# Two layers on one core: VectorE's order of sums and maxima in the units of the first layer's attention

## The reference

```python
Q = (x @ Wq.T + bq).reshape(B, S, H, dk)      # B=32, S=256, H=16, dk=8
K = ...; V = ...
scores = jnp.einsum('bqhd,bkhd->hbqk', Q, K)
attn = jax.nn.softmax(scores, axis=1)         # over b, the 32 sequences
heads = jnp.einsum('hbqk,bkhd->bqhd', attn, V)
```

## Time and profile before

| what | value |
|---|---|
| median of 3 runs | 1535.37 us (1533.78 to 1540.93) |
| the profiled execution, its own time | 1537.03 us |
| its span, first to last instruction | 1535.3 us |
| TensorE busy | 1345.0 us (88%) |
| VectorE busy | 1063.1 us (69%) |
| ScalarE busy | 821.2 us (53%) |
| GpSimd busy | 1045.2 us (68%) |
| VectorE's maxima (L847) | 128 of 2282 ns each |
| VectorE's sums (L865) | 128 of 2276 ns each |

### The profile page before, as it was taken

How to read it: one execution, slowest core, us unless ns; L and a number is a source line. 1 busy time by engine, 2 the same in 40 slices (tenths; PEclk the granted TensorE clock), 3 DMA queues, 4 the chain that set the end, 5 groups by cost and what they waited for, 6 DMA issues and landing times. The chain is left out here.

```text
span 1535.3 us, 41490 instructions
## 1 busy us (share of the span) xinstructions
PE 1345.0 (88%) x14592; PEld 1057.5 (69%) x14593; DVE 1063.1 (69%) x1847; ACT 821.2 (53%) x1820; POOL 1045.2 (68%) x763
## 2 busy tenths in 40 slices
PE   6867999999999999996699968989999699999960
PEld 4635666666666666664589966776777699999960
DVE  5638999999999999998656535756744333333329
ACT  7824777777777777775234425533344244444430
POOL 6734999999999999999344435477777444444430
PEclk9969999999999999999699979999999899999985
DMA  6876233433333443313254431011111122222228
GB/s 215 296 216 164 71 92 95 99 97 94 95 99 98 99 100 100 93 30 130 76 159 144 146 106 56 22 51 58 41 44 44 46 67 67 66 65 65 66 86 286
DMA packets 112207, 155.16 MB, mean 101 GB/s; under 512 B 17856, under 2 KB 85696, under 8 KB 107200
## 3 DMA queue, kind: packets, MB, share of 16 engines
q1 hardware_dynamic: 78496, 106.64, 25.5%
q0 software_dynamic: 13344, 27.92, 5.5%
q10 hardware_dynamic: 20224, 18.65, 3.8%
HBM read 95.33 MB, written 57.82 MB: 100 GB/s over the span
## 5 line engine op out<-in xcount | busy, mean ns | idle before, releaser
L1035 POOL TENSOR_TENSOR V<-Ex,R 128x4096 f32<-128x4096 f32 x64 | 477.3, 7458 | 14.8 <-ACT R L955 14.7
L964 ACT ACTIVATE Ex<-pB 128x512 f32<-128x512 f32 x512 | 305.2, 596 | 115.1 <-PE pB L754 96.7
L847 DVE TENSOR_REDUCE mg<-pA 128x128 f32<-128x2048 f32 x128 | 292.1, 2282 | 9.4 <-PE pA L734 9.4
L865 DVE TENSOR_REDUCE Z<-Ex 128x64 f32<-128x2048 f32 x128 | 291.0, 2276 | 7.2 <-ACT Ex L964 7.2
L1120 POOL DMA_INDIRECT y_d<-x1yb,x1xb x136 | 131.6, 968 | 151.4 <-DVE x1yb L1257 144.9
L764 PE MATMUL pO<-V,Vh 128*8 128x128 f32 x4096 | 161.8, 279 | 14.1 <-POOL V L1035 14.1
L1797 POOL DMA_INDIRECT xs_d<-d_xn,d_idx x128 | 130.9, 1023 | 42.1 <-issue 35.3
L1257 DVE COPY x1yb<-x1pY 128x128 f32<-128x128 f32 x136 | 39.7, 292 | 161.2 <-PE x1pY L1154 161.2
L749 PE MATMUL pB<-mh,identb 128*128 128x512 bf16 x386 | 148.7, 385 | 0.2
L749 PE MATMUL pB<-ml,identb 128*128 128x512 bf16 x386 | 146.5, 379 | 0.0
L1143 PE MATMUL x1pU<-x1xT,x1w1s 128*128 128x128 f32 x1088 | 145.1, 277 | 0.2 <-ACT x1xT L1181 0.2
(11 more groups left out here) (268 smaller groups left out, 2554.1 us busy)
## 6 DMA issues: line engine op xcount, KB each, us to landing
w<-qs_d SPq DMA_DIRECT2D x48, 192.0 KB
w<-ks_d SPq DMA_DIRECT2D x48, 192.0 KB
qk<-qs_d SPq DMA_DIRECT2D x48, 192.0 KB
qk<-ks_d SPq DMA_DIRECT2D x48, 192.0 KB
x1xb<-xs_d SPq DMA_DIRECT2D x136, 64.5 KB
f_ye<-y_d SPq DMA_DIRECT2D x16, 512.0 KB, 4.8
qs_d<-parts SPq DMA_DIRECT2D x16, 384.0 KB, 3.0
ks_d<-parts SPq DMA_DIRECT2D x16, 384.0 KB, 3.1
```

Source lines behind the costliest of these rows:

```text
L847: dve.tensor_reduce(mg[:, :, g], pA[:].rearrange("p b q -> p q b"), AX.X, ALU.max).then_inc(b_red, 1)
L865: dve.tensor_reduce(Z[:, j % 2, q], Ex[:, j, q, :], AX.X, ALU.add).then_inc(b_sum, 1)
L964: act.activation(Ex[:, j, :, BG * g:BG * (g + 1)], pB[:, g % 2, :, :].rearrange("p b q -> p q b"), ACT.Exp).then_inc(b_exp, 1)
L1035: pool.tensor_tensor(En[:, j % 2, :, :].rearrange("p b q -> p q b"), Ex[:, j, :, :], R[:, j % 2, :].unsqueeze(2).broadcast_to([P, P, B]), ...
```

## The change

VectorE's order within a body of the loop changes; no instruction is added or removed, and all waits stay with their instructions.

```diff
                         v, vj = u - 1, (j + 3) % 4
                         summed = j > 0 or started(h, 1)
 
+                        if summed:
+                            half_sum(v, vj, 0)
                         if more:
                             group_max(u + 2, 0)
                         if summed:
-                            half_sum(v, vj, 0)
+                            half_sum(v, vj, 1)
                         if more:
                             group_max(u + 2, 1)
                             unit_max(u + 2, (j + 2) % 4)
-                        if summed:
-                            half_sum(v, vj, 1)
```

## The result

The changed kernel is slower, as forecast, and by about the forecast amount:

| | median us | runs |
|---|---|---|
| before | 1534.59 | 4 (1533.78 to 1540.93) |
| changed | 1598.87 | 4 (1596.0 to 1603.9) |
| ratio | 1.0405 | 95% interval 1.0382 to 1.0427 |
| predicted | 1593 | range 1584 to 1605 |

The account below looks back on a forecast made before the run. VectorE was taken to bound the kernel, at 9.23 us a unit. A new wait of 0.94 us makes 10.17, and 61 units give 57.0 us more: 1593 us, range 1584 to 1605.

Parts of the forecast that it names:

- What bounds: VectorE in the attention of layer 0: busy 559.25 of 563.39 us, so reordering can win almost nothing.
- The ring: Attention loop, small maximum to cast, exponential 7 and first sum: 1.28 us where 0.34 was, 0.94 more a unit.
- The low end of the range: 1584 us: 0.15 us less a unit if the sum starts before exponential 7 ends and the cast's hand-over varies.
- The period: Attention, one small maximum to the next: 10.17 us a unit in place of 9.23, 61 times.
- TensorE keeps up: First scores of group 1 some 0.4 us later, 1.0 us left before the second maximum; not late unless its clock falls.
- GpSimd: Its multiplications in the attention do not become late; they only wait longer for R, about 0.9 us a unit.
- The clock: Rival, TensorE's clock falls in the attention: dips give 1604 (within the 0.88 case); held at 1.2 GHz, 2065, chance 0.02.
- a sign that the prediction is wrong: TensorE's clock in the attention below 1.00 would show the prediction wrong.
- The other signs on that list: Prediction wrong if small maxima stay about 9.2 us apart or exponential 7 doesn't follow the cast.
- a dip was priced at 0.16 us a unit: Before the second maximum: a 1.56 us clock dip overruns TensorE's reserve by some 0.16; 61 make 10 us, so 1604.
- The size: Whole attention stretch: 61 units of 10.17 make 620.4 us against 563.39, 57.0 us more.

Follow-up runs that it names:

- the second trace: The changed kernel run again with no edit, against the kernel before: 1596.69 us, ratio 1.0387.

## Why the prediction was right

*What bounds.* VectorE had no gap to win, and the change could only put one in. Shown: with the cast out of the way, the same new order runs at the old period, 9.24, neither faster nor slower.

*The ring.* Small maximum, cast, exponential 7, S0: forecast 1.28 us, measured 434.37 - 433.09 = 1.28. The step from ScalarE's end to VectorE's start was taken as 0.03 and is 0.04 in this unit (434.33 to 434.37). The low end of the range, a ring shorter by 0.15, wanted a sum that starts before the exponential has ended; the steps read here lie 0.03 to 0.04 behind its end (with the cast one exponential earlier, 414.24 to 414.27). The Trainium skill ("Advanced Engine Details and Errata", Miscellaneous Facts, Network/Comms) gives 50 to 100 ns for the reading of a semaphore; here the whole step is shorter, 0.04 us, and the measurement decides.

*The period.* Forecast 10.17, measured 10.19: the two steps behind the wait, S0 to M0 and M0 to S1, are 2.20 instead of 2.19. 61 x 0.02 = 1.2 us of the difference between 57.0 and the 58.3 of the second trace.

*TensorE keeps up.* Forecast: first scores of group 1 some 0.4 us later, M1 not waiting, second scores with reserve. Measured: 0.37 us of waiting for `mg` and a start 5.82 us behind the small maximum (438.91 against 433.09, forecast 5.8), no bracket before M1, and the scores of group 7 done at 432.65, 0.89 us ahead of the cast at 433.54, where the forecast has 9.7 against 10.6. ScalarE's own wait ahead of the cast is 0.92, forecast 0.9.

*GpSimd.* It waits about 1.2 us a unit for R (74.5 over 61). In the two multiplications shown the wait is 0.95 us longer than in those before (1.18 and 1.50 against 0.23 and 0.55); forecast was 0.9.

*The clock.* Forecast as a rival at its worst and as the top of the range at its mildest. In the first trace of the changed kernel it fell once, at the start of the attention: 0.61 from 155 to 165 us, where before had 0.88. That one unit took 11.61 us instead of 10.19, so 1.4 us; from 180 to 690 us the clock reads 1.00. With two pauses of 0.37 and 0.72 us a unit the clock held.

Two things were wrong here. A clock below 1.00 in the attention was named as a sign that the prediction is wrong; it reads 0.99 in both traces, from dips at the start (1.00 from 180 to 690 us). The other signs on that list came as forecast, so this one was too strict. And a dip was priced at 0.16 us a unit, ahead of M1. In the second trace, dips to 0.83 (140 to 160 us) made no unit longer than 10.20. The longer dip of the first cost 1.42 us, most of it in another place:

```profile
157.66 0.63 PE L754 MATMUL pB<-w 72*128 72x128 bf16 x4
...
158.33 0.60 ACT L964 ACTIVATE Ex<-pB 128x512 f32<-128x512 f32 x1 [0.50 <-PE pB L754]
...
158.96 2.29 DVE L865 TENSOR_REDUCE Z<-Ex 128x64 f32<-128x2048 f32 x1 [2.03 <-ACT Ex L964]
...
165.79 2.29 DVE L847 TENSOR_REDUCE mg<-pA 128x128 f32<-128x2048 f32 x1 [0.15 <-PE pA L734]
```

The scores of group 7 came so late that exponential 7 waited for them and no longer for the cast. S0 waited 2.03 us in place of 0.86, and only 0.15 of waiting stood ahead of M1. At this price a dip in every unit would have made 61 x 1.42 = 87 us, so 1605 was no bound for that rival. The time stayed inside the range because the clock held, for which the prediction had one row, 700 to 709 us.

*The size.* 57 us were forecast. The attention itself became 58.3 us longer in the second trace and 59.7 in the first, which has the unit of 11.61. The two comparisons, 1.0387 and 1.0405, make about 59 and 62 us. What lies beyond the attention's share is scatter outside it as far as the traces show it.

## What to carry to other kernels

When the order on one in-order engine is changed, look up for each moved instruction the producer it waits for, and read on in the producer's queue: what stands ahead of it there, and whether one of those waits for the engine being reordered. A round trip of that kind is paid in every turn, here 0.94 us x 61, unless other work of the engine lies between its two ends; one sum or maximum of 2.2 us was enough to cover 1.28. Before undoing such an order, see whether the foreign instruction can move instead: one digit in ScalarE's order brought the whole loss back.

## What the runs showed of the hardware that was not expected

TensorE's clock can turn a computed wait into a larger one. With the small maximum last, TensorE paused about 1.9 us ahead of each unit's second scores, and the granted clock over the attention was 0.93; in the units where it fell to the lower level, products that take 0.38 us took 0.63:

```profile
412.36 0.38 PE L754 MATMUL pB<-w 72*128 72x128 bf16 x4 [1.90 <-ACT pB L946]
...
414.12 0.63 PE L749 MATMUL pB<-ml,identb 128*128 128x512 bf16 x1
```

The 21 units of this kind lost 3.04 - 1.48 = 1.56 us each on VectorE's path, the same 1.56 that was read from the start of the attention before. Four more lost about 2.9 each, and together it was 707.33 - 61 x 10.88 = 43.65 us. With S0 alone moved, pauses of up to 1.60 us (180 to 690 us) went with a clock of 0.93 and some 10 us. With the cast one exponential earlier, pauses of 1.20 to 1.26 us went with 0.97 and some 2 us. With S1 alone moved and in the changed kernel, where no regular pause is longer than 0.8, the clock was 0.99 over the attention. The Trainium skill says ("TensorE: Matmul & The Clock Gate", What's actually happening) that activity is what releases the throttle; the traces agree with the direction. That it is the pauses, and not something else that changes with the order, is argued from these five kernels and not shown by a run of its own.
